# Expert stage of an MoE kernel: the odd slots' scatter-adds go to a second accumulator, added into the first at the end

## What is computed

```
out = sum over 32 experts e:  p[:, e] * (silu(clip(x @ wg[e].T)) * clip(x @ wu[e].T)) @ wd[e].T
out = out + the same with one shared expert, unweighted;   h = h + out
```

## Time and profile before

| | |
|---|---|
| median of 3 runs | 1386.21 us (1382.37 to 1389.91) |
| the profiled execution | 1387.62 us |
| its span, first to last instruction | 1385.5 us |
| mean granted TensorE clock, share of full speed | 0.927 |
| busy share of the span: PE, PEld, DVE, ACT, POOL | 77%, 47%, 46%, 26%, 29% |

### The profile page before, as it was taken

One profiled execution on the slowest core, in us unless ns is written; L12 is line 12 of the kernel. 1 busy time (PEld: TensorE's weight loads), 2 busy tenths in 40 slices (PEclk: granted clock), 3 DMA queues, 4 the chain that ended last, 5 costly groups with the idle time before them and its releaser, 6 DMA issues. The chain is left out here.

```text
span 1385.5 us, 22778 instructions
## 1 busy us (share of the span) xinstructions
PE 1070.7 (77%) x5648; PEld 651.1 (47%) x5649; DVE 634.3 (46%) x1459; ACT 360.6 (26%) x1030; POOL 401.1 (29%) x585
## 2 busy tenths in 40 slices
PE   0443378888868888859897599899889888988893
PEld 0343367777657777634344244344344343444341
DVE  8999644544434644464967332222222222222220
ACT  2111044454425545412100022222112122222220
POOL 0000032022021222010028435444444344534453
PEclk9766689999979999979998699999999999999997
DMA  4144400000000000020051466666667666565754
GB/s 150 26 67 77 77 1 2 1 1 1 2 2 1 1 1 1 1 70 0 1 191 52 148 188 146 162 131 199 180 169 210 190 149 173 128 160 124 212 127 77
DMA packets 51195, 124.66 MB, mean 90 GB/s; under 512 B 21664, under 2 KB 22688, under 8 KB 46384
## 3 DMA queue, kind: packets, MB, share of 16 engines
q0 software_dynamic: 19296, 47.10, 17.6%
q1 hardware_dynamic: 31824, 76.63, 17.3%
HBM read 176.35 MB, written 35.44 MB: 153 GB/s over the span
## 5 line engine op out<-in xcount | busy, mean ns | idle before, releaser
L1452 PE MATMUL ex_gu<-ex_wt,ex_xT 128*128 x680 | 331.2, 611 | 7.7 <-issue 4.8
L1576 POOL DMA_INDIRECT out_dram<-ex_ys,ex_sidx x84 | 134.1, 1596 | 242.8 <-issue 126.4
L1452 PEld LDWEIGHTS ex_gu<-ex_wt,ex_xT 128*128 128x128 f32 x680 | 123.9, 195 | 139.5 <-issue 139.5
L1519 DVE COPY ex_xT<-ex_tx 128x512 f32<-128x512 f32 x86 | 59.4, 691 | 256.7 <-PE ex_tx L1443 256.7
L1489 PE MATMUL ex_y<-ex_wt,ex_actT 128*128 x336 | 158.9, 596 | 0.0
L1511 ACT ACTIVATE ex_ys<-ex_y,ex_share 128x512 f32<-128x512 f32 x84 | 57.7, 687 | 342.1 <-PE ex_y L1489 205.5
L639 ACT ACTIVATE at_pg<-at_S,at_nmax 128x129 f32<-128x129 f32 (+1 forms) x256 | 104.9, 423 | 71.8 <-DVE at_nmax L751 63.0
L751 DVE TENSOR_REDUCE at_nmax<-at_S 128x1 f32<-128x129 f32 (+1 forms) x256 | 81.9, 353 | 78.1 <-PE at_S L519 72.5
L1546 POOL DMA_INDIRECT ex_xg<-x_rows,ex_gidx x90 | 90.4, 1005 | 73.7 <-POOL ex_gidx L1543 71.6
L1534 DVE TENSOR_TENSOR ex_act<-ex_sil,ex_uc 128x256 f32<-128x256 f32 x84 | 36.5, 434 | 163.3 <-ACT ex_sil L1505 163.3
L329 PE MATMUL ssm_ps<-ssm_v,ssm_q 64*64 64x64 f32 x1024 | 46.5, 273 | 63.6 <-DVEq L287 63.6
(11 more groups left out here) (304 smaller groups left out, 2000.2 us busy)
## 6 DMA issues: line engine op xcount, KB each, us to landing
ex_wt<-in_wexp_dram SPq DMA_DIRECT2D x89, 1536.0 KB
x_rows<-rt_xa SPq DMA_DIRECT2D x16, 272.0 KB
ssm_rows<-ssm_c SPq DMA_DIRECT2D x8, 512.0 KB, 3.8
H<-ssm_rows SPq DMA_DIRECT2D x16, 256.0 KB, 5.6
out_dram<-H SPq DMA_DIRECT2D x16, 256.0 KB
at_watt<-in_watt_dram SPq DMA_DIRECT2D x1, 1536.0 KB, 8.7
ex_xg<-x_rows,ex_gidx POOLq DMA_INDIRECT x90, 4.5
out_dram<-ex_ys,ex_sidx POOLq DMA_INDIRECT x84, 4.9
```

Source lines behind the costliest of these rows:

```text
L1452: last = M(gu[n % 2][:], xT[n % 2][:, kc, :], wt[:, bass.ds(base + kc * 2 * FF, 2 * FF)], start=(kc == 0), stop=(kc == KC - 1))
L1519: V.tensor_copy(xT[n % 2][:].rearrange("p k t -> p (k t)"), tx[:]).then_inc(tx_taken, 1)
L1576: P.indirect_dma_start(T["acc"], bass.IndirectOffsetOnAxis(ap=sidx[n % 2][:], axis=0), ys[n][:], None, compute_op=ALU.add).then_inc(scatte ...
```

## The change

A second accumulator `T["acc2"]` lies in DRAM. The route stage fills its first 2176 rows with zeros. In the expert stage even slots add to `acc`, odd ones to `acc2`. SP, not POOL, now waits for each add to land, at the end of its own slot, and counts `landed` and `sent`; POOL starts the add of slot s once the adds up to slot s-2 have landed. There are four index buffers in place of two. After the last slot SP loads `acc2` into SBUF, 17 tiles of 256 KB in three parts, and POOL adds each tile to `acc` by 17 more indirect DMAs, one part at a time, and waits for all of them.

```diff
 route_stage, SP
                 sp.dma_start(T["acc"][TOKENS:TOKENS + 128, :], zero[:, 0:DM]).then_inc(zero_done, 16)
+                for t in range(NT):
+                    sp.dma_start(T["acc2"][128 * t:128 * t + 128, :], zero[:, 0:DM]).then_inc(zero_done, 16)
                 sp.wait_ge(probs_ready, 1)
...
-                sp.wait_ge(zero_done, 32)
+                sp.wait_ge(zero_done, 32 + 16 * NT)
 expert_stage
+        rowids = sb("rowids", [128, NT], i32)
+        back = sb("back", [128, NT, DM])
+        PARTS = [range(0, 6), range(6, 12), range(12, NT)]
-        sidx = [sb(f"sidx{n}", [128, 1], i32) for n in range(2)]
+        sidx = [sb(f"sidx{n}", [128, 1], i32) for n in range(UN)]
 SP
                 sp.dma_start(ident[:], T["ident"]).then_inc(ident_ready, 16)
+                sp.dma_start(rowids[:], T["rowids"]).then_inc(rowids_ready, 16)
...
+                sp.sem_inc(landed, 2)
...
                             load(it * UN + n + AHEAD, n + AHEAD)
+                            sp.wait_ge(scattered[n % 2], (it * (UN // 2) + n // 2) * 16 + 16)
+                            sp.sem_inc(landed, 1)
+                            sp.sem_inc(sent, 1)
                 for n in range(UN):
                     sp.wait_ge(w_ready[n], turns(sp) * 16 + (32 if n < AHEAD - UN else 16))
                     sp.sem_inc(sp_turn, 1)
+                for k, part in enumerate(PARTS):
+                    for t in part:
+                        sp.dma_start(back[:, t, :], T["acc2"][128 * t:128 * t + 128, :]).then_inc(rows_back[k], 16)
 POOL
                             pool.wait_ge(sidx_ready, s + 1)
+                            pool.wait_ge(landed, s + 1)
+                            pool.sem_inc(pool_turn, 1)
                             pool.wait_ge(y_ready, s + 1 + Y_SEED)
-                            P.indirect_dma_start(T["acc"], bass.IndirectOffsetOnAxis(ap=sidx[n % 2][:], axis=0), ys[n][:],
+                            P.indirect_dma_start(T["acc2"] if n % 2 else T["acc"],
+                                                 bass.IndirectOffsetOnAxis(ap=sidx[n][:], axis=0), ys[n][:],
                                                  None, compute_op=ALU.add).then_inc(scattered[n % 2], 16)
...
-                            pool.wait_ge(scattered[n % 2], (it * (UN // 2) + n // 2) * 16 + 16)
-                            pool.sem_inc(sent, 1)
...
+                pool.wait_ge(landed, last * UN + 2)
+                pool.sem_inc(pool_turn, 1)
+                pool.wait_ge(rowids_ready, 16)
+                for k, part in enumerate(PARTS):
+                    pool.wait_ge(rows_back[k], 16 * len(part))
+                    for t in part:
+                        P.indirect_dma_start(T["acc"], bass.IndirectOffsetOnAxis(ap=rowids[:, t:t + 1], axis=0), back[:, t, :],
+                                             None, compute_op=ALU.add).then_inc(added, 16)
+                pool.wait_ge(added, 16 * NT)
```

More of the change, by code:

```diff
@@ L1359, in expert_stage @@
         sem = lambda name: ctx.enter_context(nc.semaphore("ex_" + name))
+        rowids = sb("rowids", [128, NT], i32)
+        back = sb("back", [128, NT, DM])
+        rowids_ready, added, landed = sem("rowids_ready"), sem("added"), sem("landed")
+        PARTS = [range(0, 6), range(6, 12), range(12, NT)]
+        rows_back = [sem(f"rows_back{k}") for k in range(len(PARTS))]
         ident = sb("ident", [128, 128])
@@ L1553, in take_rows_index @@
                 def take_rows_index(slot, n):
-                    P.tensor_copy(sidx[n % 2][:], slot_rows[:, bass.ds(slot, 1)]).then_inc(sidx_ready, 1)
+                    P.tensor_copy(sidx[n % UN][:], slot_rows[:, bass.ds(slot, 1)]).then_inc(sidx_ready, 1)
                 for n in range(4):
@@ L1600, in build @@
     T["x2"] = nc.dram_tensor("x2_rows", (TOKENS + 128, DM + NEXP), f32).ap()
+    T["acc2"] = nc.dram_tensor("acc2_rows", (TOKENS + 128, DM), f32).ap()
     with ExitStack() as ctx:
@@ L1649, in laid_out @@
         "rowid": row.astype(np.float32),
+        "rowids": (row + 128 * np.arange(NT)[None, :]).astype(np.uint32),
         "isrow": (row < NCH).astype(np.float32),
```

## The result

The changed kernel takes 1372.07 us (median of 8 runs, 1371.46 to 1374.17) beside 1385.17 us (1380.37 to 1392.12) for the kernel before: a ratio of 0.9906 with an interval of 0.9886 to 0.9925. It is faster by 13.1 us, 0.9%. The time lies inside the predicted range and on the predicted side, but the gain is a little under half of the 27.1 us that the sum gave.

The account below looks back on a forecast made before the run. PE was taken as the floor, with POOL's chain of adds and landings over it. 1303.0 + 9.7 + 7.0 + 0.8 + 36.9 + 1.0 = 1358.4 us, 27.1 below the 1385.5 span; 1359.1 from the median, range 1345 to 1378.

Parts of the forecast that it names:

- the closing stretch: After the last add: skipped turns and waits 9.7, loads 7.0, POOL's start 0.8, 17 adds 36.9, shared engines 1.0 us.
- What bounds the kernel now: Expert stage: PE is the floor, and POOL's chain of add, landing, next add lies over it wherever a landing is slow.
- What the stage gains: Expert stage: 83 steps fall from 564.5 us to the floor of 496.9, 67.6 us; with POOL's 7.2 us, 74.8 in all.
- POOL's tail: End of the expert stage: last add 13.1 us after its ta, first 5.9 after its own; the 7.2 us difference is gained.
- The wait on SP: SP's queue in the expert stage: later weight loads stand behind the landing wait; cost nothing, hidden under a lead of 13.8 us.
- The rival of late weights: Expert stage: held-back loads cost PE 1 us each, 31 us in all; 1390, no change. Chance 0.08.
- Zeros: SP's 17 extra stores from 606 us on: 12 us in all, nothing paid, since SP then waits 90.8 us for the probabilities.
- Row numbers: Load of rowids ahead of the first weight load, for which PE waits: 0.5 us.
- the rival of a backlog that is served faster than a lone add: Closing adds: POOL's 1.6 us sets the pace, 6.4 us less, 1353. Chance 0.20.
- Served one by one: POOL's last 17 DMAs: closing adds don't overlap; at 5.7 us spacing a time of 1418, slower. Chance 0.10.
- Bad overlap at 3 us: Closing adds: spacing of 3 us, 16 us more, 1375. Chance 0.07.
- Adds that never overlap: Adds on POOL's queue never overlap, whichever tensor they go to: the stage gains nothing, about 1493. Chance 0.03.

Follow-up runs that it names:

- The one-accumulator kernel: Changed kernel with all adds to acc, each waiting for all earlier ones, loads still held back, no zeros, row numbers or closing adds: 1340.22 us, ratio 0.968.
- The count read once: Changed kernel with the count of turns read once on all five engines instead of a flag read and branch each turn: 1358.55 us, ratio 0.9803.

## Why the prediction was right on the closing stretch and wrong on the stage

**What bounds the kernel now: right, with a cause that was missed.** POOL's chain of add and landing lay over a PE floor, and taking it away gave the forecast pattern: no wait for `share`, an add that starts when `ys` is ready, a clock of 1.00. What the prediction did not ask is why some landings took 9 us; it read "a landing is slow" as given. The one-accumulator kernel and the traces show that the slow ones shared the engines with weight loads. It also counted all of POOL's 126.4 us under "issue" as landing. At each of the 20 turns about 1.1 us of it was POOL's way through the turn of its own loop, which stood behind the landing. Moving the wait to SP removes part of both causes and, without a second accumulator, gives 45 us of the stage.

**What the stage gains: the step that failed.** "At the floor they take 83 x 5.987 = 496.9 us" took a floor from three steps that lie inside one turn of the loop. Of 83 steps 20 go over a turn. The stage took 507.93 us, so the turns cost (507.93 - 496.9) / 20 = 0.55 us each, 11.0 in all. The count read once took 8.6 of the 11.0 away and left 2.5, which shows the cause. The row that would have told it stood next in the same view, at 819.46. The rest of the sum held: the prediction put some 11 us down to stretches at the lower clock, without a row, and PE's busy time fell by 13.1 us as the clock went to 1.00. What it had wrong is that PE would then never be idle: of 52.75 us of idle time 9.25 stay, and PE's waits at the turns are 9.2.

**POOL's tail: right.** 5.9 us from the last `ta` to the last add were forecast and 5.82 measured.

**The wait on SP: nothing, right.** PE has no wait for `ex_wt` in the waits after. The rival of late weights had no part in this kernel; with one accumulator it has one, 9.7 to 20.8 us. What SP's wait does cost lies at the end of the loop, below.

**Zeros: nothing, right. Row numbers: 0.5, too low.** The first `ta` is 2.3 us later than before instead of 0.5. About 1.1 of that is the load ahead of the weights by the means above; the rest isn't assigned, since the start of the stage scatters between traces.

**The closing stretch: right in sum, in part by luck.** 60.3 us were forecast from the last add on, 60.9 measured, with terms off in both directions. The skipped turns, the waits and the program's end were taken as 9.7 us: they took 7.1 (landing at 1315.5 to the first load at 1322.56) and, behind the last landing, 5.8 (1365.9 to 1371.7), 12.9 in all. The loads and POOL's start took the 7.8 us that were forecast (1322.56 to 1330.39). The 16 spacings were 29.8 us (1330.39 to 1360.18) where 32.0 had been taken, and no 1.0 for the sharing is to be seen in them. The two landings were 4.7 and 5.7 where 4.9 each had been taken. That is 3.2 - 2.2 - 1.0 + 0.6 = 0.6 us more.

The spacing deserves its reading. The forecast took it as what one add occupies of the engines, 1.96 us, and the 1.86 that were measured are something else: POOL's own pace, 1.55 us and a gap of 0.30. The queue of the adds in the kernel after, in the 5 us from 1340 and then in the 10 us from 1345 (packets, MB, share):

```profile
q0 software_dynamic: 556, 1.01, 112.9%
...
q0 software_dynamic: 783, 1.43, 102.3%
```

An add has 144 packets. From 1340 to 1345 a backlog is worked down that the loads had left: 556 packets are 3.9 adds in 5 us, 1.3 us each. The landings say the same: the first two closing adds, issued beside the loads, take 8.0 us to land, the seventh and eighth 5.0 and 4.9, and the second to the seventh land 1.25 us apart (1340.30 to 1346.57) although they were issued 1.86 apart. From 1345 to 1355 it is 1.84 us an add, which is what POOL issues. Landings then drift from 4.9 to 5.7 us, which no row explains. So the rival of a backlog that is served faster than a lone add, with POOL setting the pace, is what happened. It was worth 2.2 us and not 6.4, because POOL's pace is 1.86 us and not 1.6. The 2.0 us of the forecast came close by luck. Why a backlog is served faster is not shown.

The Trainium skill ("DMA: Bandwidth & Descriptors", section "Anatomy of one DMA — SWDGE (gpsimd) path") fits a DMA of this path as about 2.0 us plus its bytes over 436 GB/s, which for 256 KB makes an estimate of 0.6 us of streaming. The 1.3 us of an add in the backlog are twice that and the 1.96 us of a lone add three times, so the measurement decides for adds to rows in DRAM.

**The other rivals.** Served one by one: false, adds overlap at 1.86 us. Bad overlap at 3 us: false. Adds that never overlap: false.

## What to carry to other kernels

Read a floor from a whole period of the loop, the step over its turn included, and multiply that; a turn cost 0.55 us here although PE was the bound, 0.43 of it the flag and the branch. When a wait is long only now and then, ask first what shares the resource at that moment, and where in the loop the wait stands: here the wait for a landing on another engine, which held the loads back and let POOL turn its loop meanwhile, gave four fifths of the stage's gain without a second copy, and the second accumulator brought the rest at 49.5 us for its closing. And before a second copy is paid for, ask whether the order it removes is needed at all: waiting only where two adds can touch the same row gave the whole gain in place.

## What the runs showed of the hardware that was not expected

- Accumulating indirect DMAs of 256 KB from one queue passed at 1.3 us each while a backlog lasted (556 packets in 5 us), though a lone one kept the 16 engines for 1.96 us; with the backlog gone, POOL's 1.86 us from issue to issue set the pace.
- An add that met no weight load landed in 4.5 to 5.3 us, 50 times out of 50 in the kernel before; all 21 landings over 6 us had at least 1.2 MB of loads beside them.
- Moving a load by some microseconds changes which add it collides with, not that it collides: the longest landing was 8.9, 9.3 and 6.9 us with three places for the load, and the earliest place gave the best time of the three.
- Freeing one of two engines from a branch at the turn gained 0 and 2 us, all five 13.5: they were late together, each covered by the other.
